# Softplus and the product of delta and x for chunks 1 to 7 in the main loop, and a front written anew

## What is computed

```python
xn = _layernorm(x)                                   # x: (2, 2048, 512)
s = _L0_attn_ref(xn, ...)
g = _silu(_L0_ffn_ref(xn, ...))
x = x + s * g

# _L0_attn_ref: a selective scan, 512 channels, 16 states
x_conv = silu(conv_bias + causal depthwise conv, 4 taps)
proj = einsum('btd,pd->btp', x_conv, xproj_w)        # 128 for dt, 16 B, 16 C
delta = softplus(einsum('btr,dr->btd', dt_in, dtproj_w) + dtproj_b)
a = exp(delta[..., None] * A)
b = delta[..., None] * B_in[:, :, None, :] * x_conv[..., None]
h = a_t * h + b_t                                    # over the 2048 times
y = einsum('btdn,btn->btd', h_all, C_in) + x * D_param

# _L0_ffn_ref: 8 experts, the best 2 of each token, 1024 places per expert
h = gelu(einsum('ecd,edh->ech', disp, fc1_w) + fc1_b)     # 512 -> 2048
eo = einsum('ech,ehd->ecd', h, fc2_w) + fc2_b             # 2048 -> 512
y = y + g[:, None] * eo[idx[:, s], pos_safe_l[s]]
```

## Time and profile before

| | us |
|---|---|
| median of 3 runs | 2120.51 |
| range of the runs | 2120.25 to 2121.52 |
| the profiled execution | 2124.99 |
| its span | 2123.4 |

### The profile page before, as it was taken

One profiled execution on the slowest core, in us unless ns is written; L12 is line 12 of the kernel. 1 busy time (PEld: TensorE's weight loads), 2 busy tenths in 40 slices (PEclk: granted clock), 3 DMA queues, 4 the chain that ended last, 5 costly groups with the idle time before them and its releaser, 6 DMA issues. The chain is left out here.

```text
span 2123.4 us, 30587 instructions
## 1 busy us (share of the span) xinstructions
PE 1891.6 (89%) x9064; PEld 1468.1 (69%) x9064; DVE 1829.1 (86%) x1967; ACT 1235.3 (58%) x1807; POOL 1321.6 (62%) x590
## 2 busy tenths in 40 slices
PE   6599829999999999999999999999999999999900
PEld 3233227888788788878787878787887788778800
DVE  6556649989998989898988998899888988998869
ACT  3267746566656665656565656565656566655433
POOL 1167758566856685668566866685668566856700
PEclk9899959999999999999999999999999999999955
DMA  9613354123512351235114511451245214421389
GB/s 286 254 41 98 105 217 98 65 69 130 119 65 67 132 119 63 67 135 120 60 65 138 117 62 64 140 112 68 61 142 105 75 59 144 101 79 59 70 297 380
DMA packets 89190, 246.92 MB, mean 116 GB/s; under 512 B 13296, under 2 KB 14320, under 8 KB 77808
## 3 DMA queue, kind: packets, MB, share of 16 engines
q1 hardware_dynamic: 70640, 207.30, 28.6%
q0 software_dynamic: 18176, 37.83, 9.8%
q10 hardware_dynamic: 256, 0.26, 0.1%
HBM read 173.66 MB, written 71.70 MB: 116 GB/s over the span
## 5 line engine op out<-in xcount | busy, mean ns | idle before, releaser
L1015 POOL TENSOR_TENSOR ub_sb<-u_sb,brow_sb 128x1024 f32<-128x1024 f32 x256 | 639.7, 2499 | 409.3 <-DVE a_sb L1105 406.2
L1105 DVE TENSOR_TENSOR_SCAN a_sb<-a_sb,state,ub_sb 128x512 f32<-128x512 f32 x512 | 883.7, 1765 | 9.8 <-issue 7.2
L765 PE MATMUL pm<-xTh,w1l 128*128 128x512 f32 x1024 | 425.1, 415 | 11.4 <-issue 7.0
L765 PE MATMUL pm<-w2h,hl 128*128 128x512 f32 x1024 | 422.9, 413 | 0.0
L767 PE MATMUL pm<-xTh,w1h 128*128 128x512 f32 x1024 | 403.1, 394 | 0.0
L767 PE MATMUL pm<-w2h,hh 128*128 128x512 f32 x1024 | 401.8, 392 | 0.0
L766 PE MATMUL pm<-xTl,w1h 128*128 128x512 f32 x1024 | 399.9, 391 | 0.0
L766 PE MATMUL pm<-w2l,hh 128*128 128x512 f32 x1024 | 398.5, 389 | 0.0
L1076 DVE SCALAR_TENSOR_TENSOR s_acc<-pt,ct_keep,s_acc 128x512 f32<-128x512 f32 x480 | 352.0, 734 | 24.7 <-PE pt L795 23.8
L915 ACT ACTIVATE a_sb<-delta_sb,neg_a_keep 128x512 f32<-128x512 f32 x512 | 330.1, 713 | 6.5
L795 PE MATMUL pt<-m_ident,a_sb 128*128 128x128 f32 x2048 | 307.9, 273 | 22.6 <-DVE a_sb L1105 14.7
(11 more groups left out here) (135 smaller groups left out, 2020.3 us busy)
## 6 DMA issues: line engine op xcount, KB each, us to landing
w_raw<-in_w SPq DMA_DIRECT2D x64, 1024.0 KB
brow_sb<-b_chunks SPq DMA_DIRECT2D x128, 256.0 KB, 4.7
moe_rows<-zeros_sb SPq DMA_DIRECT2D x5, 2048.0 KB, 16.8
xin_sb<-in_x SPq DMA_DIRECT2D x8, 1024.0 KB, 6.3
xn_rows<-xn_sb SPq DMA_DIRECT2D x8, 1024.0 KB, 8.6
delta_chunks<-ln_sb SPq DMA_DIRECT2D x8, 1024.0 KB
u_chunks<-u_now_sb SPq DMA_DIRECT2D x16, 512.0 KB
delta_sb<-delta_chunks SPq DMA_DIRECT2D x8, 1024.0 KB, 8.3
```

The source lines that it names most:

```text
L765: pe.matmul(out, sl, mh, start=start, stop=False)
L1015: pool.tensor_tensor(ub[:, h], u[:, 2 * h:2 * h + 2, :], brow[:, m % 2:m % 2 + 1, :].to_broadcast([P, 2, CH]), ALU.mult).then_inc(s_["bmul ...
L1105: op = dve.tensor_tensor_scan(abuf[:, m, 2 * h + k, :], abuf[:, m, 2 * h + k, :], ub[:, h, k, :], state[:, ds(col, 1)], ALU.mult, ALU.add)
```

## The change

Two DRAM tensors are new, `z_chunks` (the values before softplus) and `xs_chunks` (the convolved x).

**front** is written without hardware loops. Loads have three buffers (`RING = 3`); a load waits until the chunk three before it is normalised. DVE measures a chunk ahead of normalising. The logits come straight from matmuls with the tokens as stationary side into PSUM (`logits`), with no turn and no copy. The convolution of chunk 0 is matmuls with all four tiles; that of chunks 1 to 7 has its first tap on ACT (`first_tap`) and three taps for four tiles on DVE; the diagonals are made on Pool. The projection alternates between `pX` and `pC`, and that of chunk ch + 1 is written ahead of turns and widening of chunk ch. Of chunks 1 to 7 only z and xs are stored; softplus and u of chunk 0 alone stay in the front: ACT's part stands behind chunk 4's copies, DVE's behind all convolutions. All 64 scatters of Pool follow each other. The zeroing is no longer there.

**main_loop** computes softplus and u of chunk e + 1 during expert e, in two halves p = 0, 1 of 2 tiles of channels. At the end of quarter p, SP loads z and xs of the half into `got` (`load_zx`), the buffer of the gathered tokens. ACT computes Abs, Exp, the addition of one and Ln of tile k (`softplus(k)`) behind exp(1) and exp(3) of quarter p + 1, which waits for its input, for `soft` of the tile before and, in chunk 0, for the zeroing. DVE has three instructions for each tile in quarter p, in the steps that the table SOFT names, ahead of `add_part`; the first waits for Ln. (ACT runs about a third of a quarter ahead of DVE, so ACT's quarter p + 1 and DVE's end of quarter p are the same time.) Pool multiplies delta by xs behind its ub product i = 1 of quarter p + 1, waiting for six `soft`. SP stores both (`store_soft`) between the rows of B 2 and 3. Staging of a chunk's rows for the gathers waits until these stores have landed. In chunk 0 SP zeroes `moe_rows` behind the rows of B of quarter 0, ahead of `load_zx` and of quarter 1's weights. The vacant adds of chunk 0 are dropped. Quarters are written out, and so is the last chunk, which gathers, turns and splits no tokens for a ninth expert. In **tail** the last stores share a semaphore.

Cut to its core:

```diff
+        self.z = dram("z_chunks", (NCH, P, KT, CH))
+        self.xs = dram("xs_chunks", (NCH, P, KT, CH))
...
+        RING = 3
...
-            for r in range(0, (S + CAP) // P, 8):
-                sp.dma_start(dr.y[r * P:(r + 8) * P].rearrange("(r p) d -> p r d", p=P),
-                             zeros[:].unsqueeze(1).to_broadcast([P, 8, D])).then_inc(s_["zeroed"], 16)
...
+            for ch in range(NCH):
+                if ch > 0:
+                    sp.wait_ge(s_["silu"], KT * ch + KT)
+                    sp.dma_start(dr.xs[ch], xnT[:, ch, :, HALO:]).then_inc(s_["xs_out"], 16)
+                sp.wait_ge(s_["bc_rows"], ch + 1)
+                sp.dma_start(dr.b[ch], bcrows[0:N, ch % 2, :]).then_inc(s_[f"b_out{ch % 2}"], 16)
+                if ch > 0:
+                    sp.wait_ge(s_["z_done"], KT * ch + KT)
+                    sp.dma_start(dr.z[ch], z(ch)).then_inc(s_[f"z_out{(ch - 1) % 2}"], 16)
...
+                if ch == 0:
+                    pe.wait_ge(s_["shifted"], 1)
+                elif ch == 1:
+                    pe.wait_ge(s_["placed"], 1)
+                else:
...
+            for ch in range(NCH):
+                if ch + 1 < NCH:
+                    project(ch + 1)
                 turn_c(ch)
...
+            def first_tap(ch):
+                if ch == 1:
+                    act.wait_ge(s_["halo"], 1)
+                if ch > RING:
+                    act.wait_ge(s_["silu"], KT * (ch - RING + 1))
+                    apart(act, s_["act_at"])
+                for kt in range(KT):
+                    op = act.activation(conv[:, ch % RING, kt, :], xnT[:, ch, kt, HALO:], ACT.Identity,
+                                        bias=chan[:, kt, C_CONVB:C_CONVB + 1], scale=chan[:, kt, C_TAP + HALO:C_TAP + HALO + 1])
+                op.then_inc(s_["tap0"], 1)
...
+            def copy_z(ch):
+                if ch < RING:
+                    xn_stored(act)
+                else:
+                    act.wait_ge(s_[f"z_out{(ch - 1) % 2}"], 16 * ((ch - 1) // 2))
+                for kt in range(KT):
+                    act.wait_ge(s_["dt"], KT * ch + kt + 1)
+                    act.activation(z(ch)[:, kt, :], pT[:, kt, :], ACT.Identity, bias=chan[:, kt, C_DTB:C_DTB + 1]).then_inc(s_["z_done"], 1)
...
+                act.wait_ge(s_["z_done"], KT)
+                act.activation(ez, z(0), ACT.Abs).then_inc(s_["absz"], 1)
+                act.wait_ge(s_["absz"], 1)
+                act.activation(ez, ez, ACT.Exp, scale=-1.0).then_inc(s_["expz"], 1)
+                act.wait_ge(s_["expz"], 1)
+                act.activation(onez, ez, ACT.Identity, bias=1.0).then_inc(s_["onez"], 1)
+                act.wait_ge(s_["onez"], 1)
+                act.activation(lnz, onez, ACT.Ln).then_inc(s_["lnz"], 1)
...
-            def softplus(ch):
-                act.wait_ge(s_["soft"], 2 * ch + 2)
-                for h in HALVES:
-                    for kt in range(h.start, h.stop):
-                        act.wait_ge(s_["dt"], KT * ch + kt + 2)
...
+            for ch in range(NCH):
+                if ch + 1 < NCH:
+                    silu(ch + 1)
+                    if ch + 4 < NCH:
+                        first_tap(ch + 4)
                 copy_projection(ch)
-                silu(ch + 1)
-                store_b(ch)
                 copy_ct(ch)
-                softplus(ch)
-            copy_projection(NCH - 1)
-            store_b(NCH - 1)
...
-            for ch in range(NCH):
-                end = min(len(choices), FIRST_SCATTERS + ch * NEXT_SCATTERS)
-                for s, t in choices[begin:end]:
+            for s in range(2):
+                for t in range(NT):
                     pool.indirect_dma_start(dr.slots, bass.IndirectOffsetOnAxis(ap=place[:, s, t:t + 1], axis=0),
                                             entry[:, s, t, :], None).then_inc(s_["scattered"], 16)
-                begin = end
-                pool.wait_ge(s_["rounded"], 2 * ch + 1)
-                pool.tensor_tensor(back[:, HALVES[0]], za[:, HALVES[0]], back[:, HALVES[0]], ALU.subtract).then_inc(s_["dropped"], 1)
-                pool.wait_ge(s_["u_out"], 32 * ch + 32)
-                for n, h in enumerate(HALVES):
...
+            def convolve(ch):
+                dve.wait_ge(s_["tap0"], ch)
+                for k in range(1, TAPS):
+                    for kt in range(KT):
+                        c = conv[:, ch % RING, kt, :]
+                        if k > 1:
+                            dve.wait_ge(s_["taps"], KT * (HALO * (ch - 1) + k - 2) + kt + 1)
+                        dve.scalar_tensor_tensor(out=c, in0=xnT[:, ch, kt, HALO - k:HALO - k + CH], scalar=chan[:, kt, C_TAP + HALO - k:C_TAP + HALO - k + 1],
+                                                 in1=c, op0=ALU.mult, op1=ALU.add).then_inc(s_["taps"], 1)
...
+            with eng.Fori(1, NCH - 1) as e:
                 body(e)
+            body(NCH - 1)
...
+            for q in range(1, NQ - 1):
                 quarter(e * NQ + q, q, False, False)
-            quarter(e * NQ + NQ - 1, NQ - 1, False, True)
+            quarter(e * NQ + NQ - 1, NQ - 1, False, not ends(e))
...
+                def load_zx(p):
+                    if p == 0:
+                        sp.wait_ge(s_["x_turned"], TILES * e + TILES + 4)
+                    else:
+                        sp.wait_ge(s_["soft_out"], 64 * e + 32)
+                    for n, src in enumerate((dr.z, dr.xs)):
+                        sp.dma_start(got[:, 2 * n:2 * n + 2], src[ds(e + 1, 1), :, 2 * p:2 * p + 2, :].rearrange("o p k t -> p (o k) t")).then_inc(s_["zx_in"], 16)
+                def store_soft(p):
+                    sp.wait_ge(s_["soft"], 12 * e + 6 * p + 6)
+                    sp.dma_start(dr.delta[ds(e + 1, 1), :, 2 * p:2 * p + 2, :].rearrange("o p k t -> p (o k) t"), got[:, 0:2]).then_inc(s_["soft_out"], 16)
+                    sp.wait_ge(s_["u_done"], 2 * e + p + 1)
+                    sp.dma_start(dr.u[ds(e + 1, 1), :, 2 * p:2 * p + 2, :].rearrange("o p k t -> p (o k) t"), got[:, 2:4]).then_inc(s_["soft_out"], 16)
...
+                        if not begins(e):
+                            sp.wait_ge(s_["soft_out"], 64 * e)
...
                         for tb in range(TPC):
                             store_s(tb)
-                    for m in range(2, NPQ):
-                        load_b(it, q, m)
+                    load_b(it, q, 2)
+                    if q in (1, 2) and not ends(e):
+                        store_soft(q - 1)
+                    load_b(it, q, 3)
+                    if first and begins(e):
+                        sp.wait_ge(s_["cleared"], 4)
+                        for r in range(0, (S + CAP) // P, 8):
+                            sp.dma_start(dr.y[r * P:(r + 8) * P].rearrange("(r p) d -> p r d", p=P),
+                                         expz[:].unsqueeze(1).to_broadcast([P, 8, D])).then_inc(s_["zeroed"], 16)
+                    if q in (0, 1) and not ends(e):
+                        load_zx(q)
...
+                    def softplus(k):
+                        p = q - 1
+                        n = 4 * e + 2 * p + k
+                        if k == 0:
+                            act.wait_ge(s_["zx_in"], 64 * e + 32 * p + 32)
+                            if begins(e) and p == 0:
+                                act.wait_ge(s_["zeroed"], 16 * ((S + CAP) // P // 8))
+                        if not (begins(e) and p == 0 and k == 0):
+                            act.wait_ge(s_["soft"], 3 * n)
+                        apart(act, s_["act_at"])
+                        act.activation(expz[:], got[:, k, :], ACT.Abs).then_inc(s_["absz"], 1)
+                        act.wait_ge(s_["absz"], n + 1)
+                        act.activation(expz[:], expz[:], ACT.Exp, scale=-1.0).then_inc(s_["expz"], 1)
+                        act.wait_ge(s_["expz"], n + 1)
+                        act.activation(onez[:], expz[:], ACT.Identity, bias=1.0).then_inc(s_["onez"], 1)
+                        act.wait_ge(s_["onez"], n + 1)
+                        act.activation(b2[:], onez[:], ACT.Ln).then_inc(s_["lnz"], 1)
+                    if not (first and begins(e)):
...
+                        if q in (1, 2) and not ends(e) and i in (1, 3):
+                            softplus(i // 2)
...
+                if not begins(e):
+                    pool.wait_ge(s_["soft_out"], 64 * e)
+                    apart(pool, s_["pool_at"])
...
+                        if q in (1, 2) and not ends(e) and i == 1:
+                            pool.wait_ge(s_["soft"], 12 * e + 6 * (q - 1) + 6)
+                            pool.tensor_tensor(got[:, 2:4], got[:, 0:2], got[:, 2:4], ALU.mult).then_inc(s_["u_done"], 1)
...
+                        if first and not begins(e):
...
+                    def softplus(k, part):
+                        n = 4 * e + 2 * q + k
+                        if part == 0:
+                            dve.wait_ge(s_["lnz"], n + 1)
```

(11 more changed lines are left out.)

491 lines of the change are left out of this document (205 added, 286 removed).

## The result

| | before | after |
|---|---|---|
| median, runs of both side by side | 2121.02 us (4 runs) | 2266.34 us (4 runs) |
| range | 2120.25 to 2122.67 | 2251.10 to 2269.45 |
| ratio, 95% interval | | 1.0669 [1.0636, 1.0703] |
| the profiled execution, and its span | 2124.99, 2123.4 | 2263.8, 2261.9 |

The change makes the kernel 145 us slower: 101 more than the 2165 that was forecast, and outside the range. The direction was right and so was the first link of the mechanism; the sizes were not.

What follows compares the result with a forecast made beforehand. PE bounds the loop with DVE close beside it, so PE pays added DVE time one for one. Front -75, end -4, chunk 0 +27, six chunks +96 give +44: 2169 profiled, 2165 median; own case 2112 to 2205, overall range 2095 to 2205.

Steps and rivals of the forecast that it cites:

- DVE's wait: Loop, quarter 0, step 11: DVE arrives at 783.19 and stands until Ln is done at 793.0, 9.8 us.
- PE's wait behind it: Loop, quarter 0, step 15: PE needs the bank of a part queued behind DVE's wait and idles 6 us.
- the wait for the second tile's Ln: Loop, quarter 0: the second softplus ends at 801.1 and DVE, there at 800.3, waits 0.9 us.
- the zeroing: Chunk 0: 10.5 MB of zeros on the SP queue ahead of z, x and quarter 1's w1 cost +24 us.
- only the last gap is followed by critical work: +1.6: Loop, quarter 0 into 1: gaps lower PE's clock, but only the last one's slow restart costs time, 1.6 us.
- +3.3, less what quarter 1's slower clock gives: Loop, quarter 1 into 2: scans 1 end near 864.9, PE's transposes want them at 861.6, so at most 3.3 us.
- rival (a): Loop: the stall doesn't reach PE; 0 to 6 us a chunk, 5 to 15 for chunk 0, total 2070; chance 0.14.
- not the main cost: Loop, quarter 0 into 1: the six DVE softplus instructions matter less than when their input comes.
- its logits at 60.5: Front: the last chunk is normalised at 52 us, its logits stand at 60.5, and the places at 82.
- (b): Loop: PE pays step 15's 6 us and half the rest, 8 or 9 a chunk, total 2115 to 2125; chance 0.14.
- (c): Front: savings shrink to 50 us through saturated DMA engines and PE's lower clock in gaps, total 2190; chance 0.12.
- the bound of 20 a chunk: Loop, chunks 1 to 6: upper bound of the added time per chunk, taken as 16 us, lower bound 11.

Runs made afterwards that it cites:

- e4: After with the zeroing back in the front, from a tile of its own, and no waits for it in the loop: 2277.77 us against 2131.01 of before.
- e1: After with all softplus and u work left out of the main loop, loads and stores too: 2149.78 us against 2131.01 of before.
- e7: e4 with ACT's softplus left out of the loop, DVE's and Pool's instructions kept: 2256.97 us against 2125.95 of before.
- e13: e7 with DVE's softplus at ends of odd steps, stores behind the next first weights, Pool's product and last quarter's first gathers later: 2199.85 us against 2130.62 of before.
- e2: After with the logits as before, transposed, by 512-column matmuls with a copy and turns: 2274.48 us against 2131.01 of before.
- e14: e12 with DVE's softplus at ends of odd steps (second tile's three in step 25), stores behind the next first weights: 2169.44 us against 2125.93 of before.
- e12: After with old logits, zeroing in front, scatters spread, ACT's second tile behind first gelus, DVE's softplus in steps 15 to 25, product later: 2267.07 us against 2134.11 of before.
- e10: e7 with DVE's six instructions spread over steps 1 to 9 of the next quarter, Pool's product at its end: 2339.39 us against 2134.11 of before.
- e6: After unchanged, run again: 2301.73 us against 2125.95 of before.

## Why the prediction was wrong

**Right.** ACT's schedule; DVE's wait (9.8 forecast, 9.96 measured); PE's wait behind it (6, 6.04); the wait for the second tile's Ln (0.9, 0.67) and none at the second half's instructions; the zeroing (+24 forecast, 27.6 by e4); the work added to DVE in a chunk (twelve instructions of 0.75, two products that block a scan for 1.2 each, and 0 to 4.3 of further blocking make 11.4 to 15.7; measured 12.4, of which 8.7 is blocking on the new instructions, less 4.0 on the scans, which is within what the scans vary by, so the closeness of the sum is in part luck); and in the front the 22 us of routing, the rounds to within 1.6 us each and the softplus of chunk 0.

**Wrong, the loop.** The forecast's terms by quarter, against what the chunk shows:

| | forecast | measured | PE idle | PE's work slower |
|---|---|---|---|---|
| quarter 0 | 6 | 10.6 | +6.0 | +4.6 |
| quarter 1 | 6 + 1.6 | 6.4 | +3.2 | +3.2 |
| quarter 2 | 3.3 | 7.1 | +5.1 | +2.0 |
| quarter 3 | 0 | 2.4 | +2.4 | 0 |
| chunk | 16.9, taken as 16 | 26.6 | +16.8 | +9.8 |

The step that failed in quarter 0 is the clock's: "only the last gap is followed by critical work: +1.6". Each gap of 2 us or more leaves six to eleven matmuls at the 1.2 GHz level, 0.2 us lost on each, 1.5 us a gap, and there are five: some 8 of the 9.8 us. Of quarter 0's 4.6, 2.7 come from the gap at the edge (e1 and e7 have them without any wait for Ln) and the rest from the gap of 6.04. The slow matmuls are time that PE pays itself; besides, DVE, when it comes out of its own wait, waits for PE (6.2 us in quarter 0 instead of 1.2) and then lets PE wait again. DVE's idle time outside the wait for Ln, 18.5 us a chunk before, did not take up anything; it became 22.2. How much of the 9.8 us would have turned into idle time had the clock stayed up, no run shows: in quarter 1 DVE is full in any case.

In quarter 2 the failed step is "+3.3, less what quarter 1's slower clock gives". DVE has 15.6 us more work in quarters 1 and 2 (57.26 + 54.99 against 51.18 + 45.44), and 7.3 us of idle time to put it in, of which 5.2 stay idle between its waits for PE and ACT. And quarter 1's figure came out near the mark by luck, for a wrong reason. I had put 6 of its 7.6 us down to the aftermath of the Ln wait; e7 has no such wait, and its quarter 1 is no shorter (60.4 us; e4 with the wait 59.4). The sharpest refutation is that of rival (a)'s price. A chunk without the wait was to grow by 0 to 6 us; e7's grew by 21.6, and e13's, with the instructions in the best places that I found, by 14.5 (the edge between chunks, below, in both). The six DVE instructions of a half, which I called "not the main cost", are, with Pool's blocking, the main cost.

The Trainium skill (SBUF — State Buffer, section SBUF: two separate sides), which the forecast weighed, says that a VectorE instruction with two SBUF inputs and a GpSimd one that reads SBUF exclude each other for the whole instruction. The rows agree: 0.69 us alone, 1.81 behind a product, 5.00 behind a subtraction. I had applied it to the subtraction of quarter 1 alone; six of the twelve instructions of chunk 2 are held up.

**Wrong, the edge.** Quarter 3's 2.4 us and the low clock at the start of quarter 0 come from a gap of 4.2 instead of 1.75 us between chunks, for which no term stood. The runs show what it is not, and that it goes with the new logits; its cause stays open. A rough split of the 26.6: the edge 3.8 to 5.7 (e2, e1), the wait for Ln 5.1 (e7 against e4), and some 16 to 18 for DVE's twelve instructions, with the blocking and the clock behind the gaps that they make. The last part is what is left over, and no run takes out these instructions alone.

**Chunk 0 and the end.** 37.7 instead of 27: the zeroing 27.6 instead of 24; quarters 1 and 2 another 14.6, where the forecast had 3 in quarter 2; and quarter 0 without the zeroing 4.8 less, for which no term stood. The peeled chunk gave back 8.0 us at the end, not 4; which of the dropped steps does it wasn't looked into.

**Wrong, the front.** -43 instead of -75. The step "its logits at 60.5" failed: 28.7 us late, 17 by the eight-column matmuls and their clock (e2), 3.1 by later normalising and 8.5 because PE, not the chain of loads and normalising, is the bound there. The three slow rounds, 4.8 us, cover the rest. I had costed the new logits by the turns and copies that they save, and not by their own 256 matmuls of eight columns with a weight load each, which no row of before showed and which should have widened the range.

**Rivals.** (a), an absorbed stall, falls with the rows at 815.64 and 818.56, and (b), a stall paid in part, with a chunk that grew by 26.6 and not by 8 or 9. (c) named the front's shortfall, for another reason, but kept the loop. None had the loop's size: the bound of 20 a chunk came from the one event of each kind that I followed, not from how often it would recur.

## What to carry to other kernels

Where two engines are both near nine tenths busy, as here, cost added work or a wait on one of them as a series: the gap, the other's slow start after it, and the first one's wait for that. Idle time elsewhere took up little. Place DVE instructions with two SBUF inputs where Pool is idle, and count the scans that Pool then blocks instead (e14 against e12, 15 us a chunk with the same instructions in the loop, SP's order included). And a store behind a late product must not stand on SP's queue ahead of the next weights (12.31 us of PE in e10).

## What the runs showed of the hardware

- Matmuls of eight columns, each with its weight load, with turns of 128 columns between them, kept PE busy 28.00 of 28.00 us at a granted clock of 0.50; with 512-column ones in their place (e2) it was 0.94 to 1.00. Busy records are no assurance of the full clock.
- A row of 64 indirect scatters from Pool went, in nine of the ten profiles of kernels that have it, with ACT almost and PE wholly at rest for 25 to 50 us; in e6 the DMA engines were at a share of 0.09 meanwhile. It is open why.
- The same loop, differing only in what lies ahead of it in the program, has a gap between iterations of 1.6 or of 4.2 us on PE (e2 and after). In all 15 traces the long gap goes with the new logits in the front. Also open.
